# A rotary mixture attention block: the order of the first head, of four products a head and of the angle tiles

## What is computed

```python
q, k, v = x @ wq, x @ wk, x @ wv              # 16 query heads; k and v shared by 4 each
logits = (x @ wr).reshape(B, N, H, 4)
tk_vals, tk_idx = top_k(logits, 2)
member = one_hot(tk_idx).sum(-2) > 0
pos = cumsum(member) - member                 # a position per node
for n in range(4):
    qr = q * cos[pos[n]] + rotate_half(q) * sin[pos[n]]     # k likewise
    scores = where(causal & member[n], qr @ kr.T / 8, -1e9)
    outs.append(softmax(scores) @ v)
y = (softmax(tk_vals)[..., None] * gathered(outs, tk_idx)).sum() @ wo
```

## Time and profile before

| | us |
|---|---|
| three runs | 920.02, 923.35, 923.91 (median 923.35) |
| profiled execution | 922.07, span 920.3 |
| TensorE busy | 827.7 (90%), 6552 matrix products |
| weight loads of TensorE | 580.7 (63%) |
| VectorE busy | 790.6 (86%) |
| ScalarE busy | 734.3 (80%) |
| GpSimd busy | 607.2 (66%) |
| range mask of head 1 to that of head 63 | 76.59 to 787.41 |

### The profile page before, as it was taken

How to read it: one execution, slowest core, us unless ns; L and a number is a source line. 1 busy time by engine, 2 the same in 40 slices (tenths; PEclk the granted TensorE clock), 3 DMA queues, 4 the chain that set the end, 5 groups by cost and what they waited for, 6 DMA issues and landing times. The chain is left out here.

```text
span 920.3 us, 21302 instructions
## 1 busy us (share of the span) xinstructions
PE 827.7 (90%) x6552; PEld 580.7 (63%) x6552; DVE 790.6 (86%) x1996; ACT 734.3 (80%) x2001; POOL 607.2 (66%) x951
## 2 busy tenths in 40 slices
PE   4459989999999999999999999999999999999893
PEld 4346656666666666666666666666666667575793
DVE  6869978998899889988998899889988888787895
ACT  6258898889888988898888888888888887865572
POOL 4556778776877677767776777677656666128492
PEclk9779999999999999999999999999999999999997
DMA  9101111121111121112121211121101110323553
GB/s 209 42 16 24 38 29 37 36 40 31 38 37 36 32 41 37 36 32 40 37 37 31 40 38 37 30 39 32 15 9 16 17 14 14 126 70 93 149 168 113
DMA packets 81039, 45.01 MB, mean 49 GB/s; under 512 B 35072, under 2 KB 79808, under 8 KB 80928
## 3 DMA queue, kind: packets, MB, share of 16 engines
q1 hardware_dynamic: 79712, 41.15, 20.3%
q0 software_dynamic: 1216, 2.51, 0.8%
HBM read 30.62 MB, written 12.43 MB: 47 GB/s over the span
## 5 line engine op out<-in xcount | busy, mean ns | idle before, releaser
L1543 PE MATMUL psum<-QK 128*128 128x128 f32 (+3 forms) x1024 | 369.8, 453 | 5.2 <-DMA wrow<-words 4.4
L768 ACT ACTIVATE probs<-psum,negmax 128x128 f32<-128x128 f32 (+3 forms) x512 | 266.8, 528 | 56.0 <-DVE negmax L1128 32.4
L530 POOL TENSOR_TENSOR R<-pcs 128x512 f32<-128x512 f32 x128 | 176.3, 1399 | 49.6 <-DVE pcs L1087 49.6
L1543 PEld LDWEIGHTS psum<-QK 128*128 128x128 f32 x1024 | 159.2, 192 | 51.0 <-issue 46.8
L556 POOL TENSOR_TENSOR coef<-rden,wslot 128x2 f32<-128x2 f32 x256 | 53.3, 208 | 173.4 <-DVE rden L1134 173.3
L1139 DVE SCALAR_TENSOR_TENSOR accs<-probs,coef,accs 128x128 f32<-128x128 f32 (+3 forms) x256 | 164.5, 643 | 2.5 <-ACT accs L777 2.5
L777 ACT ACTIVATE accs<-probs,coef 128x128 f32<-128x128 f32 (+3 forms) x256 | 148.0, 578 | 17.6 <-POOL coef L556 17.3
L1087 DVE TENSOR_TENSOR pcs<-psum,arena 128x512 f32<-128x512 f32 x256 | 161.7, 672 | 0.0
L1556 PE MATMUL psum<-ident,accs 128*128 128x128 f32 x640 | 115.9, 279 | 26.5 <-ACT QK L745 20.3
L1128 DVE CUSTOM_DVE_ANT_0 psum<-psum,outside 128x512 f32<-128x512 f32 x128 | 87.8, 700 | 51.9 <-PE psum L1545 51.2
L745 ACT ACTIVATE QK<-psum 128x384 f32<-128x384 f32 x235 | 116.1, 494 | 1.1 <-PE psum L1530 1.1
(11 more groups left out here) (272 smaller groups left out, 1558.2 us busy)
## 6 DMA issues: line engine op xcount, KB each, us to landing
weight_halves<-whl SPq DMA_DIRECT2D x48, 128.0 KB, 2.2
arena<-weight_halves SPq DMA_DIRECT2D x22, 256.0 KB, 3.1
wrow<-words SPq DMA_DIRECT2D x64, 86.0 KB
arena<-weight_halves SPq DMA_DIRECT2D x7, 512.0 KB, 6.7
wrow<-words SPq DMA_DIRECT2D x64, 42.0 KB
wst<-in_L_ffn_w_up_dram SPq DMA_DIRECT2D x14, 128.0 KB, 2.4
wst<-in_L_ffn_w_gate_dram SPq DMA_DIRECT2D x14, 128.0 KB, 2.4
wst<-in_L_ffn_w_down_dram SPq DMA_DIRECT2D x14, 128.0 KB, 2.5
```

What stands on the lines that cost most here:

```text
L530: pool.tensor_tensor(R[u][:, :, :, 0:3:2, half * HALF:(half + 1) * HALF].rearrange("p t e j f -> p (t e) j f"), halves(pc, half), halves(p ...
L768: act.activation((expB if e else expA)[:, k % (4 if e else 3), 0:w], area, ACT.Exp, scale=1.0 if k % TB < 2 else -1.0, bias=negmax[k % 4][ ...
L1543: pe.matmul(o, QK[:, u, e, rows], QK[:, u, 2, 0:w], start=True, stop=False)
```

## The change

Head 0 is rotated by VectorE in the opening (`first_rotation`: the ten instructions of `rotate` and of the code gaps, in one sequence behind the four products), with GpSimd starting at head 1. The mask words are made right behind the angles' sizes and written to DRAM ahead of the mask rows; the product with the logits moves ahead of the angles' sizes. The first two heads' scores wait for the mask row only. The Exp table is loaded right after the first cosines, and the mixing weights are made behind the first exponentials (`mix_weights`, same instructions). The last two products of head 1, the first range mask, the projection of head 2 and the transposition of step 4 are issued later.

In the heads with even `n`, without the table step, the four products of head `n + 2` are issued as one, two and one at `s = 0`, 1 and 2, and there GpSimd issues the coefficients before part 0 of the rotation. The angle tiles of tables 2 to 7 go to the odd heads; those of table 1 stay in heads 0 to 3. Value projections behind the first take a bank in turn (`v`) instead of `psM`.

```diff
         def angle_tile(k):
             n, s = k // TB, k % TB
-            if s == 1 and n % SPAN < TB and n // SPAN + 1 < NH // SPAN:
-                return n // SPAN * TB + n % SPAN
-            return None
+            if s != 1 or n >= (NH // SPAN - 2) * SPAN + TB:
+                return None
+            if n < TB:
+                return n
+            return n // SPAN * TB + (n % SPAN - 1) // 2 + 2 if n % 2 and n >= SPAN - 3 else None
+        def spread(n):
+            return n % 2 == 0 and n % SPAN != TB
+        def products_at(k):
+            n, s = k // TB, k % TB
+            if n + 2 >= NH:
+                return ()
+            if n == 0:
+                return (((1, 2), (1, 3)), ((2, 0), (2, 1)), ((2, 2), (2, 3)), ())[s]
+            of = (((0,), (1, 2), (3,), ()) if spread(n) else ((0, 1), (2, 3), (), ()))[s]
+            return [(n + 2, which) for which in of]
...
+            if k % TB == 2 and k // TB % GROUP == 2 and k // TB // GROUP + 1 < B * KV:
+                turns.append(("v", k // TB // GROUP + 1))
...
+        def value_bank(g):
+            return turn_bank(("v", g)) if g else psM
...
@@ sync
-            sp.wait_ge(S["mk_ev"], 8)
+            sp.wait_ge(S["words_done"], 1)
+            for b in range(B):
+                sp.dma_start(words_d[b * H:(b + 1) * H, :], words[b * 2 * H:b * 2 * H + H, :]).then_inc(S["zero_done"], 16)
+            sp.wait_ge(S["mk_ev"], 6)
             sp.wait_ge(S["zeros_done"], 2 * RING + 1)
             for n in range(RING):
                 head_masks(n)
-            sp.wait_ge(S["words_done"], 1)
-            for b in range(B):
-                sp.dma_start(words_d[b * H:(b + 1) * H, :], words[b * 2 * H:b * 2 * H + H, :]).then_inc(S["zero_done"], 16)
             sp.wait_ge(S["zero_done"], 16 * (2 + B))
             for n in range(RING):
+                sp.wait_ge(S[f"mm_in{n}"], 16)
                 head_words(n)
+            sp.wait_ge(S["mk_ev"], 8)
             for n in range(RING, NH):
                 sp.wait_ge(S["scores_done"], 2 * TB * (n - RING + 1))
+                sp.wait_ge(S["masked"], 2 * (n - RING + 1))
                 head_masks(n)
-                sp.wait_ge(S["masked"], 2 * (n - RING + 1))
                 head_words(n)
@@ gpsimd
+                if k == 0:
+                    pool.wait_ge(S["w_done"], 2)
                 pool.wait_ge(S["rden_done"], k + 1)
...
-            for part in range(4):
-                rotate(0, part)
             rotate(1, 0)
+            pool.wait_ge(S["k_done"], 1)
             rotate(1, 1)
-            pool.wait_ge(S["w_done"], 2)
...
                 m, part = (n + 2, s - 2) if s >= 2 else (n + 1, s + 2)
-                if m < NH:
+                late = part == 0 and spread(n)
+                if m < NH and not late:
                     rotate(m, part)
                 if k >= 1:
                     coefficients(k - 1)
+                if m < NH and late:
+                    rotate(m, part)
@@ scalar
             trigonometry(0)
+            act.preload_act_table(ACT.Exp)
...
-            act.wait_ge(S["w_step"], 3)
...
-            act.preload_act_table(ACT.Exp)
...
             keep_qk(0)
+            act.wait_ge(S["hs_lo"], SPLITS)
...
                 if k < STEPS:
                     exponentials(k)
+                if k == 0:
+                    mix_weights()
@@ vector
             dve.tensor_tensor(dif, sA, sB, ALU.subtract).then_inc(S["w_step"], 1)
+            dve.wait_ge(S["w_step"], 1)
+            dve.tensor_tensor(dif, dif, L, ALU.mult).then_inc(S["w_step"], 1)
...
+            dve.wait_ge(S["mk_t"], 3)
+            dve.tensor_scalar(words[:, :], bank[5][:, :], -1.0, float(WORD), ALU.mult, ALU.add).then_inc(S["words_done"], 1)
...
+                if a >= TB:
+                    dve.wait_ge(S["prod_done"], 4 * SPAN * (a // TB))
...
+            first_rotation()
             dve.wait_ge(S["w_step"], 2)
             dve.tensor_reduce(lmax[:, 0, :], dif, AX_X, ALU.add).then_inc(S["w_step"], 1)
-            for e in range(2):
-                products(1, e)
+            for which in range(2):
+                product(1, which)
...
-                if k == 0:
+                if k == 1:
                     place_outside(0)
...
-                if s < 2 and n + 2 < NH:
-                    products(n + 2, s)
+                for m, which in products_at(k):
+                    product(m, which)
@@ tensor
-                    mm_ = three(psM[:, tb * HD:(tb + 1) * HD], rows_of(b, tb),
+                    mm_ = three(value_bank(g)[:, tb * HD:(tb + 1) * HD], rows_of(b, tb),
...
-            pe.wait_ge(S["mk_ev"], 8)
-            pe.wait_ge(S["prod_done"], 8)
-            project(2)
...
-                pe.wait_ge(S[f"mm_in{r}"], 48 * (n // RING + 1))
+                pe.wait_ge(S[f"mm_in{r}"], 48 * (n // RING + 1) if n >= RING else 16)
...
                     scores(k)
-                if k + 2 < STEPS:
+                if k == 3:
+                    flip(4)
+                if k + 2 < STEPS and k != 2:
                     flip(k + 2)
...
-                    pe.wait_ge(S["prod_done"], 4 * (n + 3))
+                    wait_turn(pe, ("v", n // GROUP + 1))
                     project_value(n // GROUP + 1)
...
+                if k == 1:
+                    pe.wait_ge(S["prod_done"], 8)
+                    project(2)
                 if s == 3 and n + 3 < NH:
                     pe.wait_ge(S["prod_done"], 4 * (n + 3))
...
-                    pe.wait_ge(S["v_ev"], min(B * KV, (n + 2) // GROUP + 1))
```

More of the change, by code:

```diff
@@ L1091, in _, with product @@
-            for e in range(2):
-                products(0, e)
-            dve.wait_ge(S["mk_t"], 3)
-            dve.tensor_scalar(words[:, :], bank[5][:, :], -1.0, float(WORD), ALU.mult, ALU.add).then_inc(S["words_done"], 1)
-            dve.wait_ge(S["w_step"], 1)
-            dve.tensor_tensor(dif, dif, L, ALU.mult).then_inc(S["w_step"], 1)
+            def product(n, which):
+                e, (i, dst) = which // 2, ((1, pc), (0, ps))[which % 2]
+                if which == 0:
+                    dve.wait_ge(S["qk_mm"], n + 1)
+                    dve.wait_ge(S["trig_done"], TB + 1 + 2 * (n // SPAN))
+                    if n >= 1:
+                        dve.wait_ge(S["add_done"], 2 * n)
+                src = psM.rearrange("p (t j f) -> p t j f", t=TB, f=HALF)
+                table = trig[:, n // SPAN % 2, i, n % SPAN, :, e, :]
+                dve.tensor_tensor(dst[:, :, e, :].rearrange("p t (j f) -> p t j f", f=HALF), src,
+                                  table.unsqueeze(2).to_broadcast([P, TB, 4, HALF]), ALU.mult
+                                  ).then_inc(S["prod_done"], 1)
@@ new lines, in first_rotation, with halves, over_slot @@
+            def first_rotation():
+                tiles = slice(0, TB)
+                def halves(t_, a):
+                    return t_.rearrange("p t e (j a f) -> p (t e) j a f", j=2, a=2)[:, :, :, a, :]
+                def over_slot(t_):
+                    return t_.unsqueeze(2).to_broadcast([P, TB, HD])
+                for which in range(4):
+                    product(0, which)
+                dve.wait_ge(S["code_e"], 2)
+                dve.tensor_tensor(lmax[:, 1, :], code[:, :, 0], code[:, :, 1], ALU.subtract).then_inc(S["gap_done"], 1)
+                dve.wait_ge(S["prod_done"], 4)
+                for half, op in ((0, ALU.subtract), (1, ALU.add)):
+                    dve.tensor_tensor(R[0][:, :, :, 0:3:2, half * HALF:(half + 1) * HALF].rearrange("p t e j f -> p (t e) j f"),
+                                      halves(pc, half), halves(ps, 1 - half), op).then_inc(S["add_done"], 1)
+                dve.wait_ge(S["gap_done"], 1)
+                dve.scalar_tensor_tensor(cgap[:, :], lmax[:, 1, :], 6.0, lmax[:, 1, :], ALU.add, ALU.mult
+                                         ).then_inc(S["gap_done"], 1)
+                dve.wait_ge(S["add_done"], 2)
+                dve.tensor_tensor(kdif[:, :, :], R[0][:, :, 0, 2, :], R[0][:, :, 1, 2, :], ALU.subtract).then_inc(S["kd_done"], 1)
+                dve.wait_ge(S["gap_done"], 2)
+                dve.tensor_scalar(cgap[:, :], cgap[:, :], 11.0, -1.0 / 6.0, ALU.add, ALU.mult).then_inc(S["codes_done"], 1)
+                dve.tensor_tensor(R[0][:, :, :, 1, :], R[0][:, :, :, 0, :], codes4[:, tiles, 0, :].unsqueeze(3).to_broadcast([P, TB, 2, HD]),
+                                  ALU.mult).then_inc(S["q_done"], 1)
+                dve.wait_ge(S["kd_done"], 1)
+                dve.wait_ge(S["codes_done"], 1)
+                dve.tensor_tensor(ktok[0][:, :, 1, :], kdif[:, :, :], over_slot(gaps3[:, tiles, 0]), ALU.mult).then_inc(S["k2_done"], 1)
+                dve.wait_ge(S["k2_done"], 1)
+                dve.tensor_tensor(kcod[:, :, :], ktok[0][:, :, 1, :], over_slot(codes4[:, tiles, 0, 0]), ALU.mult).then_inc(S["kt_done"], 1)
+                dve.wait_ge(S["kt_done"], 1)
```

(1 more changed line is left out.)

34 lines of the change are left out of this document (9 added, 25 removed).

## The result

Four executions of the changed kernel took 956.72 to 966.75 us (median 964.36) against 920.02 to 923.91 (median 922.42) of the kernel before: a ratio of 1.045, 95% interval 1.0423 to 1.0477. The profiled one took 964.67, span 962.9. The forecast was 935, and its range ended at 946: the sign was right, the size was not.

What follows compares the result with a forecast made beforehand. The prediction took each pair of heads to be set by a chain from GpSimd's coefficients through ScalarE's weighing to TensorE's transposition. Terms -5.3 - 3 + 0 + 20.9 = +12.6 on 922.07 gave 934.7 us, rounded 935; range 906 to 946.

Steps and rivals of the forecast that it cites:

- opening: Heads 0 to 3: first scores about 58.2 instead of 64.92, part given back; 5.3 us gained, bounds 2.5 and 6.7.
- tiles in odd heads: Six spans move two angle tiles each from even to odd heads, where they are cheaper: 3 us gained, bounds 0 and 6.
- values in a turn bank: Value projections wait for an earlier transposition's eviction instead of the products: zero, bounds plus or minus 3 us.
- one, two, one: the waits: In 22 even heads the fourth product ends 2.2 us later, delaying adds, third-row coefficients and transposition: 20.9 us lost.
- Late coefficients: Likeliest case: third-row coefficients come late on GpSimd, holding ScalarE and then TensorE; 934.7 us (927 to 945), chance 0.58.
- I take 0.95, the free adds: Delay per even head taken from 0.95 to 1.35 us, assuming only the short weighing stands beside GpSimd's adds.
- One slack: Before the change, ScalarE weighed the third row 0.79 us after its coefficients were ready.
- the slack used up in head 14: Before the change, two extra GpSimd copies there: coefficients ready at 239.31, ScalarE weighs at 239.41, TensorE 0.37 us idle.
- the sum by the rule: Shared-port blocking would hold the second add some 0.3 us: delay some 1.25 us per even head, 27 us in all.
- rival of coefficients in time: Third-row coefficients not late if adds start within 0.8 us of before; only the 0.35 us wait goes: 906 us, chance 0.26.
- third rival: TensorE's idle stretch grows to 1.6 to 2 us; clock drops in 22 odd heads, 35 us more: 970, chance 0.07.
- likeliest case: Third-row coefficients late in 22 even heads, transposition 0.95 us later in each: 934.7 us, 927 to 945, chance 0.58.

Runs made afterwards that it cites:

- the kernel with even products: The changed kernel with products two and two in every head and the adds of even heads ahead of the coefficients again: 918.81 us, ratio 0.9981.
- the one with the wait filled: The changed kernel with second-row transpositions of rotated queries made eight times in odd heads behind spread heads: 950.49 us, ratio 1.0303.
- both waits were gone: Products two and two, old value bank, tile in head 6, plus head 1's last products earlier and head 0's coefficients early, against the kernel before: 911.71 us, ratio 0.9888.

## Why the prediction was right in sign and wrong in size

The medians of runs that differ by one part give the terms; they add up to the whole (921.85 to 964.36):

| part | forecast | measured | from |
|---|---|---|---|
| opening | -5.3 (-2.5 to -6.7) | -0.9 | 921.85 to 920.95 |
| tiles in odd heads | -3 (0 to -6) | -3.1 | to 917.84 |
| values in a turn bank | 0 (3 either way) | +1.0 | to 918.81 |
| one, two, one: the waits | +20.9 | +31.7 | to 950.49 |
| the clock in those waits | none (a rival: up to +35) | +13.9 | to 964.36 |

By the intervals of two runs together each term is known to 1.5 to 3 us, so only the tiles and the last two stand clear of zero. The traces bear those two out: from the kernel with even products to the one with the wait filled the 22 pairs of heads grow by 30.8 us, and without the filling the eleven slow heads are 17.9 us longer (the profiles as a whole differ by 13.6, since the one with the filling starts its first head 2.5 us later and takes 1.6 longer behind the last).

**Late coefficients.** The chain was right at every link: second row in time, adds 2.09 us later (forecast 2.2), ScalarE held for the third row, TensorE behind it. The step that failed is its size, "I take 0.95, the free adds". In a pair without a tile it is 1.14, with one 1.36 (9.67 + 13.65 against 10.18 + 11.78), and over the 22 heads 31.7 us between medians, 1.44 each, just over the upper bound of 1.35. One slack, that of head 46, had been taken for all: the pairs of the heads 6 to 15 grew by 1.7 to 1.9, where the forecast itself had seen the slack used up in head 14. The coefficients came 1.99 us behind the adds' end, not 1.7: the code product took 1.26 us, against 1.04 with even products, as it began at 760.72 while VectorE weighed (760.61). The Trainium skill's rule on the shared port (SBUF — State Buffer, "Who interferes with whom") agrees with that row, where GpSimd is the one held: in this trace the ten code products that began during a weighing took 1.27 us in the median, the forty with none beside them 1.04. The forecast placed the collision at an add, and there the trace does not bear it out: the weighing took 0.34 us (759.17), as long as with no GpSimd work beside it, and the two adds 2.58 (forecast 2.49). That the sum by the rule, 27 us, was nearer than 20.9 by the rows alone is therefore partly luck.

**The order counted as a help.** The forecast credited "GpSimd makes the second row's coefficients first" with the end of a wait of 0.35 us, and let the fourth product alone set the adds' start. Beside the moved product both hold: the adds wait a last 0.39 us for the product, and without the order the kernel is 12.3 us slower (976.70). Not seen was that the order is a gate of its own, 19.9 us by itself: it puts ready adds behind a wait for a reciprocal that comes at nearly the same moment as the fourth product. The two gates overlap and their losses do not add up. The rival of coefficients in time (0.26) fell by its own condition: the adds start 2.09 us later, and it allowed 0.8.

**The clock.** The third rival was given 0.07 and left outside the range; all that stood for so little was that the stretch lay between one of 1.24 us, behind which the clock stayed, and one of 2.21, behind which it did not. The stretches came out at about 2 us, as that rival had it, and the clock fell in 11 of the 22 odd heads and cost 1.4 to 1.7 us in each, as that rival priced it (the mean granted clock of the four executions was 0.957 to 0.982, lowest in the slowest, 966.75 us, and highest in the fastest, 956.72). So the likeliest case and this rival were not alternatives: the wait of the one is the cause of the other, and with the measured delay (31.7) and half of 35 the forecast's own sum would have been 963. The range was also narrower than its terms: their upper bounds together give 952 us (922.07 - 2.5 + 0 + 3 + 29.7), not 945.

**The opening.** The gain was summed up at the fifth step's scores (70.1 forecast, 69.63 measured), and all behind was taken to follow at the same distance. Head 1 did not: the first rows' coefficients stood behind the rotation of head 1 on GpSimd, a queue that the forecast followed for the rotation and not for its coefficients. Head 1 was also at a clock of 0.92 with the opening alone, and at full clock, 11.15 us, once both waits were gone. In the profiled executions of the edited kernels, which are alike up to there, the opening reaches TensorE's first angles up to 3 us apart (41.15 to 44.20), so one profile can't size it and the medians do.

**The tiles** were right within the error, by an even part (pairs of 21.96 instead of 22.59) less one that was not foreseen, the second wait in head 5 of the first span, at a clock of 0.80.

## What to carry to other kernels

On an engine with an in-order queue, putting a short instruction first also puts its wait first: before moving it ahead, ask when its input comes and what ready work then stands behind it. Where a forecast makes TensorE wait as long as in rows behind which the clock has fallen (about 2 us here), count the clock as a consequence of the wait and not as a rival to it; a stretch that can't be closed may be worth filling with work whose result is thrown away. And a gain at the front of a pipeline is not counted until the same distance is seen one head later on every queue.

## What was not expected of the hardware

The clock fell behind idle stretches of 1.95 us (heads 47 and 51, then 0.50 of full speed, 1.2 GHz) and stayed at 2.4 GHz behind others of 2.12 (head 57) and 2.59 (head 9). In head 5 the same wait of 2.2 us is in every kernel's trace, and without the tile the clock stayed in three and fell in three. Length alone does not decide, and what does was not settled here. The Trainium skill (TensorE: Matmul & The Clock Gate, "HAM oscillation — how this bites in real kernels") tells of waits, longer than these, that lower the clock anew in every tile; this trace agrees for half of the odd heads, and in the other half the clock stayed. And adding 336 transpositions made the changed kernel 13.9 us faster.
